# Graph network, first layer: one gather in 18 groups fetched row by row from ScalarE's queue

## The chip, the cores and the metric

One core of one Trainium2 chip runs the kernel. Times are device microseconds (us) of one execution; the time of a kernel is the median over its runs. The engines are PE (TensorE), DVE (VectorE), ACT (ScalarE), POOL (GpSimd) and SP (SyncE). A DMA is issued by SP, ACT or POOL and carried out by 16 DMA engines that they share.

## The reference

A graph of 6250 nodes with 128 features and 200,000 edges, sorted by destination. The change is in the first layer:

```python
h = x @ W1 + b1
e = concatenate([h[dst], h[src] - h[dst]])        # per edge, 256 wide
m = relu(e @ W2 + b2)
m = relu(m @ W3 + b3)
out = relu(segment_max(m, dst))
x = layernorm(x + out)
```

Two graph attention convolutions over the same edges follow (the "second layer" below, two passes), with softmax weights per destination, and another layernorm.

## The kernel before, in words

`e @ W2` splits into a part of the destination, P = h (W2a - W2b) + b2, and a part of the source, Q = h W2b. Both are made once per node; Q lies in HBM as `Q_table`, one row of 512 bytes a node. Then the edges are worked off in chunks of 128: 1563 chunks in 197 groups of 8 (the last three are smaller), and each group in two quads of 4 chunks, 391 quads in all (`groups`, `quads`). Three groups of six quads are a round; 64 rounds are full.

For each chunk the rows Q[src] must come into `q_ring`, which has three slots of a group each (group g uses slot g % 3).

- POOL (`gather_q`) gathers a chunk with one indirect DMA of 128 rows (line 485). Before group g it waits until PE has placed the last quad of group g-3 (`placed`).
- For the last chunk of every third group (`q_picks`, slot 2) there is no gather. PE picks its rows out of Q by products with one-hot matrices, from codes that ACT makes (`code_row`) and one-hots that DVE makes, in pieces spread over the round (`pick_piece`).
- SP (`load_windows`) loads for each chunk a window of 128 rows of P, 64 KB, into `w_ring`. It reads four window starts into registers (line 334) and issues four DMAs (line 338). Each adds 16 to `w_landed` of the slot.
- PE, in quad i: `place(i)` transposes the rows of Q into PSUM and adds the windows times a one-hot matrix; it waits for `q_landed` and `w_landed` of the whole group. Then `multiply(i-1)` by W3, then `turn_back(i-2)`, the transposes after the running maximum. In front of `multiply(i-1)` ACT must have made the ReLU of quad i-1.
- ACT, in quad i: `relu_quad(i)` (line 648), in the last quad of a round `code_row`, in every even quad the load of the ranks of a later group (line 663, 512 KB) and the store of a finished group (line 669, 512 KB), then `evacuate(i-2)` (line 655).
- DVE makes the one-hots and runs the maximum along the edges (`scan_quad`).

ACT's program is written out quad by quad. PE's runs rounds 2 to 62 in one hardware loop whose semaphore values are computed in registers.

The second layer already has row fetches of this kind, on SP: `fetch_rows` reads up to 12 row numbers into registers (line 377) and issues one DMA for each row into `one_rows` (line 381); when all 128 have landed, `move_rows` copies them into the ring with one DMA.

Of the kernel before, what the change touches and what calls it, by code (L numbers as in the profile page):

```python
# [7 lines left out]
I32 = mybir.dt.int32  # L8
# [4 lines left out]
P = 128  # L13
# [25 lines left out]
def totals(slots, amounts):  # L39

    so_far, out = {}, []
    for slot, amount in zip(slots, amounts):
        so_far[slot] = so_far.get(slot, 0) + amount
        out.append(so_far[slot])
    return out


def edge_network(nc, t, out):
    N, F = t["x"].shape
    L = t["src"].shape[1]  # L50
    NB = -(-N // P)
    NP = NB * P
    FULL, REST = N // P, N % P

    G, RING, RINGB, RINGO, AHEAD = 8, 3, 4, 3, 2
    G1, RING1, PIECE = 8, 3, 7
    PIECES = -(-NB // PIECE)
    W = F + 2
# [3 lines left out]
    groups, groups1 = cut(L, G, 4), cut(L, G1, 5)  # L62
# [15 lines left out]
    with ExitStack() as ctx:  # L78
        def sb(name, shape, dt=F32):
            return ctx.enter_context(nc.sbuf_tensor(name, shape, dt))  # L80

        def sem(name):
            return ctx.enter_context(nc.semaphore(name))
# [12 lines left out]
        src_row = sb("src_row", [P, 3, P], I32)  # L96

        one_src, one_rows = sb("one_src", [1, P], I32), sb("one_rows", [P, W])
        x_sb = sb("x_sb", [P, NB, F])

        work = sb("work", [P, NP + 7 * 512])
# [95 lines left out]

        q_picks = {RING * r + RING - 1: r - 2 for r in range(2, ROUNDS)}
        NQPICK = len(q_picks)
        pieces_after = {1: (0, 1), 2: (2,), 3: (3, 4), 4: (5,), 5: (6,)}  # L200
        by_product = [g for g, (j0, j1) in enumerate(groups1) if j1 - j0 == G1 and g >= 2]
        picks = {g: i for i, g in enumerate(by_product)}
# [5 lines left out]
        assert SHARE * (TURN - 1) >= P and all(g in picks for g in by_row) and TURN % RING1 == 0  # L208


        q_value = totals([g % RING for g in range(NG)], [16 * (j1 - j0 - (g in q_picks)) for g, (j0, j1) in enumerate(groups)])
        w_value = totals([g % RING for g in range(NG)], [16 * (j1 - j0) for j0, j1 in groups])
        b_value = totals([g % RINGB for g in range(NG)], [16] * NG)
        o_value = totals([g % RINGO for g in range(NG)], [16] * NG)
        by_dma = [(j0, j1 - (g in picks) - (g in by_row)) for g, (j0, j1) in enumerate(groups1)]
# [28 lines left out]
        h_landed = [sem(f"h_slot{i}") for i in range(RING1)]  # L244
        row_landed = [sem(f"src_row{i}") for i in range(3)]
        one_ready, one_landed = sem("one_ready"), [sem(f"one_rows{i}") for i in range(2)]

        tabs_stored, compact_zeroed, p_scattered, ranks_stored = (
            sem(n) for n in ("tabs_stored", "compact_zeroed", "p_scattered", "ranks_stored"))
# [204 lines left out]
        def pool_program(pool):  # L454
# [25 lines left out]
            def gather_q(g):  # L480
                j0, j1 = groups[g]
                if g >= RING:
                    pool.wait_ge(placed, last_of[g - RING] + 1)
                for j in range(j0, j1 - (g in q_picks)):
                    pool.indirect_dma_start(  # L485
                        out=q_ring[:, g % RING, j - j0, :], out_offset=None, in_=Q_table,
                        in_offset=bass.IndirectOffsetOnAxis(ap=srcT_i[:, j:j + 1], axis=0)).then_inc(q_landed[g % RING], 16)
# [77 lines left out]
        def scalar_program(scalar):  # L565
# [60 lines left out]
            def load_q_row(at):  # L626

                if at >= 2:
                    scalar.wait_ge(coded, at - 1)
                j = (RING * (at + 3)) * G - 1  # L630
                scalar.dma_start(src_row[:, row_slot[at], :], flat_src[j:j + 1, :].to_broadcast([P, P])).then_inc(row_landed[row_slot[at]], 16)
# [18 lines left out]
            def evacuate(i):  # L650
                g, a, n = quads[i]
                if a == 0 and g >= RINGO:
                    scalar.wait_ge(o_stored[g % RINGO], o_value[g - RINGO])
                scalar.wait_ge(turned_back, i + 1)
                scalar.activation(o_ring[:, g % RINGO, a:a + n, :],  # L655
                                  ps[4 + i % 2][:, 0:n * P].rearrange("p (c f) -> p c f", f=F), ACT.Copy).then_inc(evacuated, 1)
# [9 lines left out]
            def store_max(g):  # L666
# [2 lines left out]
                scalar.dma_start(run_max.rearrange("(c p) f -> p c f", p=P)[:, j0:j1, :],  # L669
                                 o_ring[:, g % RINGO, 0:j1 - j0, :]).then_inc(o_stored[g % RINGO], 16)  # L670

            scalar.wait_ge(ranks_stored, 32)
            scalar.wait_ge(q_low, PIECES)
            for g in range(RINGB):
                load_ranks(g)
            load_q_row(0)
            load_q_row(1)
            scalar.wait_ge(p_scattered, 16 * NB)
            for i in range(NQ + 3):
                turn, step = divmod(i, ROUND)  # L680
                if i < NQ:
                    relu_quad(i)
                    if step == ROUND - 1 and turn < NQPICK:
                        code_row(turn)
                    if step == 0 and 1 <= turn < NQPICK - 1:
                        load_q_row(turn + 1)
                    if quads[i][1] == 0 and RINGB <= quads[i][0] + AHEAD < NG:
                        load_ranks(quads[i][0] + AHEAD)
                if i >= 3 and last_of[quads[i - 3][0]] == i - 3:
                    store_max(quads[i - 3][0])  # L690
                if 2 <= i < NQ + 2:
                    evacuate(i - 2)

            def root(at, n):

# [535 lines left out]
        def tensor_program(tensor):  # L1231
# [66 lines left out]
            def place(q, count, i, landed, loaded, added):  # L1298

                g, a, n = quads[q]  # L1300
                if q >= 2:
                    tensor.wait_ge(relued, count[i - 1])
                tensor.wait_ge(q_landed[g % RING], landed)
                tensor.wait_ge(w_landed[g % RING], loaded)
                tensor.wait_ge(onto_made, count[i + 1])
                if g in q_picks and a + n == G:
                    tensor.wait_ge(row_added, added)
                for c in range(n):
                    piece = ps[q % 2][:, c * P:(c + 1) * P]
                    tensor.matmul(piece, lhsT=q_ring[:, g % RING, a + c, :], rhs=ident[:, :], start=True, stop=False, is_transpose=True)  # L1310
                    m = tensor.matmul(piece, lhsT=w_ring[:, g % RING, a + c, :], rhs=onto[:, q % 3, c * P:(c + 1) * P],  # L1311
                                      start=False, stop=True)
                m.then_inc(placed, 1)
# [48 lines left out]
            for i in range(ROUND, 2 * ROUND):  # L1362
                step(i)
                for c in pieces_after.get(i - ROUND, ()):
                    pick_piece(c, c + 1, None)
            with tensor.Fori(2, ROUNDS - 1) as turn:
                loaded, fewer = tensor.snap(turn * (16 * G) + 16 * G), tensor.snap(turn * (16 * G - 16) + 16 * (G + 1))
                added, made = tensor.snap(turn - 1), tensor.snap(turn * PIECES - PIECES)
                at = tensor.snap(turn * ROUND)
                count = {c: tensor.snap(at + c) for c in range(-3, ROUND + 1)}  # L1370
                for p in range(ROUND):
                    q = 2 * ROUND + p
                    place(q, count, p, fewer if quads[q][0] in q_picks else loaded, loaded, added)
                    multiply(q - 1, count, p - 1)
                    turn_back(q - 2, count, p - 2)
                    for c in pieces_after.get(p, ()):
                        pick_piece(c, made + (c + 1), added)
            for i in range(ROUND * (ROUNDS - 1), NQ + 2):
                step(i)

# [105 lines left out]
```

## Time and profile before

| | |
|---|---|
| median of 3 runs | 5880.39 us (5874.37 to 5883.29) |
| the profiled execution | 5872.45 us, its span 5871.2 us |
| first layer's gathers (line 485) | 1501, the last one at 2037.34 us |
| granted TensorE clock, mean | 0.94 of full speed |
| busy | PE 84%, DVE 70%, POOL 75%, ACT 45% of the span |

The span is the time from the first instruction to the last; the execution's own time holds a little more. Durations come from this one execution. Busy shares don't count register, semaphore and DMA-issuing instructions; on the queues (ACTq, SPq) these are shown in rows of their own. "issue" is time in which an engine waited for nothing that the profile shows.

### The profile page before, as it was taken

Reading aid. Unit: us, or ns where it says so; the run is one execution under the profiler, and the core shown is the slowest. Engines: PE = TensorE matmul, PEld = TensorE weight load, DVE = VectorE, ACT = ScalarE, POOL = GpSimd, SP = SyncE. Lnnn points to the kernel's source line nnn. Section 1 sums busy time; section 2 is a strip of 40 time slices with the busy share of each in tenths; the row PEclk is TensorE's granted clock in tenths of the full one; section 3 lists DMA queues with packets and bytes.
Section 4 is the critical chain, followed back from the end, with each engine's and each line's share of the span. In section 5 each row is a group of like instructions: output and inputs, shape, how many; then the busy total and the mean of one; then the engine's idle time right before and its main releaser. Section 6 shows DMA issues by size and latency. Waiting matters only on the chain.

```text
span 5871.2 us, 119756 instructions
## 1 busy us (share of the span) xinstructions
PE 4931.6 (84%) x29429; PEld 3060.9 (52%) x29429; DVE 4098.0 (70%) x10676; ACT 2658.7 (45%) x8225; POOL 4399.4 (75%) x4585
## 2 busy tenths in 40 slices
PE   3688888888888729999999999943999999999991
PEld 2566666666666525555555555522555555555550
DVE  4344454444445448888888888864888888888886
ACT  2233333333333235555555555533555555555554
POOL 7777777777777677777777777767777777777775
PEclk6899999999999959999999999976999999999995
DMA  6677777777777724444444444432444444444442
GB/s 157 187 219 217 215 223 216 217 219 217 220 217 216 202 59 120 123 124 122 124 125 124 125 124 124 125 92 63 124 123 124 124 125 124 124 124 121 125 125 83
DMA packets 808269, 874.81 MB, mean 149 GB/s; under 512 B 133438, under 2 KB 635185, under 8 KB 807818
## 3 DMA queue, kind: packets, MB, share of 16 engines
q0 software_dynamic: 146016, 295.63, 19.7%
q1 hardware_dynamic: 390298, 361.70, 18.8%
q10 hardware_dynamic: 271504, 213.69, 13.9%
q14 instruction: 440, 3.60, 0.2%
q8 instruction: 11, 0.18, 0.0%
HBM read 536.74 MB, written 331.81 MB: 148 GB/s over the span
## 4 chain that ended last, share of the span: by engine, by line
POOL 51%; issue 21%; DVE 9%; PE 7%; DMA 6%; ACT 3%; DVEq 0%; POOLq 0%; SPq 0%; ACTq 0%
POOL ring_a L545 25%; POOL ring_a L485 22%; DMA ring_a<-H_table,src_i 6%; PE ps L1417 5%; DVE ring_b L1120 5%; ACT ring_a L746 2%; POOL ring_a L512 2%; POOL ad_edges L520 2%; POOL P_compact L498 1%; PE ps L1311 1%; DMA ring_a<-Q_table,src_i 1%; DVE ring_a L1074 1%; PE ps L1321 1%; DVE gz L1104 1%; DVE ring_b L1074 0%
## 5 line engine op out<-in xcount | busy, mean ns | idle before, releaser
L545 POOL DMA_INDIRECT ring_a<-H_table,src_i x2712 | 2588.2, 954 | 826.9 <-issue 755.9
L1417 PE MATMUL ps<-work,ring_a 128*128 128x390 bf16 x10752 | 1867.3, 330 | 238.5 <-DVE ring_a L1074 234.9
L485 POOL DMA_INDIRECT ring_a<-Q_table,src_i x1501 | 1432.8, 955 | 461.0 <-issue 453.0
L1417 PEld LDWEIGHTS ps<-work,ring_a 128*128 128x128 bf16 x10752 | 1015.8, 98 | 1065.2 <-DVE ring_a L1074 387.7
L1417 PE MATMUL ps<-work,ring_b 128*128 128x390 bf16 x8064 | 1407.7, 329 | 0.0
L638 ACT ACTIVATE code<-src_row,code_bias 128x128 int16<-128x128 int32 x2676 | 829.5, 389 | 1214.2 <-DVE ring_b L1074 1152.0
L1120 DVE SCALAR_TENSOR_TENSOR ring_b<-ring_b,gw,ring_a 128x129 f32<-128x129 f32 x3124 | 1092.0, 350 | 120.4 <-ACT ring_a L746 104.2
L948 DVE TENSOR_TENSOR_SCAN work<-ring_b,work,ps 128x512 f32<-128x512 bf16 x390 | 498.4, 1278 | 951.8 <-PE ps L1321 911.1
L1417 PEld LDWEIGHTS ps<-work,ring_b 128*128 128x128 bf16 x8064 | 787.0, 98 | 559.7
L746 ACT ACTIVATE ring_a<-ring_a,gw 128x129 f32<-128x129 f32 x3126 | 959.3, 390 | 0.0
L1074 DVE TENSOR_TENSOR ring_a<-code,ps 128x896 bf16<-128x896 int16 x1536 | 944.1, 615 | 1.2 <-issue 0.3
L648 ACT ACTIVATE work<-ps 128x512 f32<-128x512 f32 x391 | 233.4, 597 | 1091.1 <-PE ps L1311 1069.6
L1310 PE MATMUL ps<-ident,ring_a 128*128 128x128 f32 x1563 | 446.5, 286 | 321.1 <-issue 164.6
L1074 DVE TENSOR_TENSOR ring_b<-code,ps 128x896 bf16<-128x896 int16 x1152 | 706.8, 614 | 0.0
L1311 PE MATMUL ps<-work 128*128 128x128 f32 x3126 | 567.1, 284 | 0.0
L1311 PEld LDWEIGHTS ps<-work 128*128 128x128 f32 x3126 | 501.4, 202 | 3.6 <-issue 0.3
L1310 PEld LDWEIGHTS ps<-ident,ring_a 128*128 128x128 f32 x1563 | 228.8, 146 | 391.3 <-issue 342.0
L1321 PE MATMUL ps<-work,W 128*128 128x512 f32 (+1 forms) x782 | 423.3, 625 | 0.0
L655 ACT ACTIVATE tab_flat<-ps 128x512 f32<-128x512 f32 x391 | 232.1, 594 | 262.6 <-PE ps L1331 259.0
L1331 PEld LDWEIGHTS ps<-ident,work 128*128 128x128 f32 x1563 | 202.3, 145 | 222.3 <-issue 221.2
L1101 DVE TENSOR_TENSOR gz<-ring_a,ad_wide 128x8 f32<-128x8 f32 (+2 forms) x394 | 70.3, 178 | 301.0 <-DMA ring_a<-H_table,src_i 291.5
L740 ACT ACTIVATE gw<-gw 128x16 f32<-128x16 f32 (+2 forms) x394 | 85.0, 216 | 384.0 <-DVE gw L1114 384.0
(267 smaller groups left out, 3625.2 us busy)
## 6 DMA issues: line engine op xcount, KB each, us to landing
run_sum<-ring_b SPq DMA_DIRECT2D x388, 520.0 KB
work<-P_compact SPq DMA_DIRECT2D x1563, 64.0 KB
ring_b<-rank_rows ACTq DMA_DIRECT2D x194, 512.0 KB, 5.2
run_max<-tab_flat ACTq DMA_DIRECT2D x194, 512.0 KB
one_rows<-H_table SPq DMA_DIRECT2D x3840, 0.5 KB
ring_a<-H_table,src_i POOLq DMA_INDIRECT x2712
src_row<-in_srcL SPq DMA_DIRECT2D x384, 64.0 KB, 3.0
ring_a<-Q_table,src_i POOLq DMA_INDIRECT x1501
```

The costliest lines, as they stand in the source:

```text
L485: pool.indirect_dma_start(out=q_ring[:, g % RING, j - j0, :], out_offset=None, in_=Q_table, in_offset=bass.IndirectOffsetOnAxis(ap=srcT_i[ ...
L545: pool.indirect_dma_start(out=h_ring[:, g % RING1, j - j0, :], out_offset=None, in_=H_table, in_offset=bass.IndirectOffsetOnAxis(ap=src_i[ ...
L638: scalar.activation(code[:, c, :], src_row[:, row_slot[at], :], ACT.Identity, bias=code_bias[:, c:c + 1])
L648: scalar.activation(m1T[:, b, 0:n * P], ps[b][:, 0:n * P], ACT.Relu).then_inc(relued, 1)
L746: scalar.activation(h_ring[:, slot, i, 0:F + 1], h_ring[:, slot, i, 0:F + 1], ACT.Copy, scale=gw[:, par, 0, i:i + 1]).then_inc(scaled, 1)
L948: vector.tensor_tensor_scan(scanned[:, b, 0:n * P], b_ring[:, g % RINGB, 1, a * P:(a + n) * P], ps[2 + b][:, 0:n * P], initial, ALU.add, A ...
L1074: vector.tensor_tensor(hot_space[c // 4][:, c % 4, 0:k1 - k0, :], code[:, c:c + 1, :].to_broadcast([P, k1 - k0, P]), blocks_ps[:, 0:k1 - k ...
L1120: vector.scalar_tensor_tensor(out=r_ring[:, slot, i, 0:F + 1], in0=previous, scalar=gw[:, par, 1, i:i + 1], in1=h_ring[:, slot, i, 0:F + 1 ...
L1310: tensor.matmul(piece, lhsT=q_ring[:, g % RING, a + c, :], rhs=ident[:, :], start=True, stop=False, is_transpose=True)
L1311: m = tensor.matmul(piece, lhsT=w_ring[:, g % RING, a + c, :], rhs=onto[:, q % 3, c * P:(c + 1) * P], start=False, stop=True)
L1321: tensor.matmul(ps[2 + b][:, 0:n * P], lhsT=weights["W3"][:, :], rhs=m1T[:, b, 0:n * P], start=True, stop=True).then_inc(multiplied, 1)
L1417: m = tensor.matmul(ps[parity][:, 0:3 * W], lhsT=hot_space[c // 4][:, c % 4, k - k0, :], rhs=split[:, k, :, :].rearrange("p s f -> p (s f) ...
```

## The change

Nine groups, 18, 36, ..., 162 (`q_by_row`, all in slot 0), lose the gather of their last chunk. ACT fetches its 128 rows instead. `list_q_few` loads the chunk's 128 source numbers into one partition (`few_src`). Over the first 32 of the 36 quads of a turn of 18 groups, `fetch_q_few` reads four numbers into registers behind the quad's evacuation and issues four DMAs of one row each into `few_rows`. In quad 34 `move_q_few` waits for all 128 rows and copies them with one DMA of 64 KB into the slot of the ring, and the next turn's list is loaded. The copy counts on `w_landed`, so PE waits for it there. There is no tenth turn: from quad 324 on ACT does what it did.

Since the expected values of `q_landed` and `w_landed` of slot 0 now step once in six rounds, PE's loop of 61 rounds becomes three: rounds 2 to 5; 8 super turns of 6 rounds, nested; and rounds 54 to 62. The body (`round_of`) is the same, with two more values in registers.

```diff
+        few_src, few_rows = sb("few_src", [1, P], I32), sb("few_rows", [P, W])
...
+        QTURN, QROWS = 18, 4
+        QTURNS = RING * ROUNDS // QTURN
+        q_by_row = [QTURN * i for i in range(1, QTURNS)]
...
-        q_value = totals([g % RING for g in range(NG)], [16 * (j1 - j0 - (g in q_picks)) for g, (j0, j1) in enumerate(groups)])
-        w_value = totals([g % RING for g in range(NG)], [16 * (j1 - j0) for j0, j1 in groups])
+        q_value = totals([g % RING for g in range(NG)], [16 * (j1 - j0 - (g in q_picks) - (g in q_by_row)) for g, (j0, j1) in enumerate(groups)])
+        w_value = totals([g % RING for g in range(NG)], [16 * (j1 - j0 + (g in q_by_row)) for g, (j0, j1) in enumerate(groups)])
...
-                for j in range(j0, j1 - (g in q_picks)):
+                for j in range(j0, j1 - (g in q_picks) - (g in q_by_row)):
                     pool.indirect_dma_start(
...
+            def list_q_few(turn):
+
+                j = groups[q_by_row[turn]][1] - 1
+                scalar.dma_start(few_src[:, :], flat_src[j:j + 1, :]).then_inc(q_listed, 16)
+
+            def fetch_q_few(turn, e0):
+
+                g = q_by_row[turn]
+                if e0 == 0:
+                    scalar.wait_ge(q_listed, 16 * (turn + 1))
+                    if turn:
+                        scalar.wait_ge(w_landed[g % RING], w_value[g - QTURN])
+                _, row = nc.values_load_multi_w_load_instructions(
+                    few_src[0:1, e0:e0 + QROWS], engines=[scalar.engine], min_val=0, max_val=NP - 1,
+                    skip_runtime_bounds_check_because="sources are numbers of nodes")
+                for d in range(QROWS):
+                    scalar.dma_start(few_rows[e0 + d:e0 + d + 1, 0:F], Q_table[bass.ds(row[d], 1), :]).then_inc(q_few_landed, 16)
+
+            def move_q_few(turn):
+
+                g = q_by_row[turn]
+                scalar.wait_ge(q_few_landed, 16 * P * (turn + 1))
+                scalar.wait_ge(placed, last_of[g - RING] + 1)
+                scalar.dma_start(q_ring[:, g % RING, G - 1, :], few_rows[:, 0:F]).then_inc(w_landed[g % RING], 16)
...
+            list_q_few(0)
             scalar.wait_ge(p_scattered, 16 * NB)
...
                 if 2 <= i < NQ + 2:
                     evacuate(i - 2)
+                turn_q, p = divmod(i, 2 * QTURN)
+                if turn_q < QTURNS - 1 and p * QROWS < P:
+                    fetch_q_few(turn_q, p * QROWS)
+                if turn_q < QTURNS - 1 and p == 2 * QTURN - 2:
+                    move_q_few(turn_q)
+                    if turn_q + 1 < QTURNS - 1:
+                        list_q_few(turn_q + 1)
...
-            with tensor.Fori(2, ROUNDS - 1) as turn:
-                loaded, fewer = tensor.snap(turn * (16 * G) + 16 * G), tensor.snap(turn * (16 * G - 16) + 16 * (G + 1))
+
+            def round_of(turn, first, windows):
+
+                loaded = tensor.snap(turn * (16 * G) + 16 * G)
+                fewer = tensor.snap(turn * (16 * G - 16) + 16 * (G + 1))
...
-                    place(q, count, p, fewer if quads[q][0] in q_picks else loaded, loaded, added)
+                    g = quads[q][0]
+                    place(q, count, p, (first, loaded, fewer)[g % RING], loaded if g % RING else windows, added)
...
+            each = QTURN // RING
+            with tensor.Fori(2, each) as turn:
+                round_of(turn, tensor.snap(turn * (16 * G) + 16 * G), tensor.snap(turn * (16 * G) + 16 * G))
+            with tensor.Fori(1, QTURNS - 1) as super_turn:
+                with tensor.Fori(0, each) as i:
+                    within = tensor.snap(i * (16 * G) + 16 * G)
+                    round_of(tensor.snap(super_turn * each + i), tensor.snap(super_turn * (16 * G * each - 16) + within),
+                             tensor.snap(super_turn * (16 * G * each + 16) + within))
+            with tensor.Fori(each * (QTURNS - 1), ROUNDS - 1) as turn:
+                round_of(turn, tensor.snap(turn * (16 * G) + (16 * G - 16 * (QTURNS - 1))),
+                         tensor.snap(turn * (16 * G) + (16 * G + 16 * (QTURNS - 1))))
```

## Rows read from the trace of the kernel before

**Rows 1.** Page, 1: busy time of each engine, share of the span, instructions
```profile
PE 4931.6 (84%) x29429; PEld 3060.9 (52%) x29429; DVE 4098.0 (70%) x10676; ACT 2658.7 (45%) x8225; POOL 4399.4 (75%) x4585
```

**Rows 2.** Page, 4: the chain that ended last, by engine and by line
```profile
POOL 51%; issue 21%; DVE 9%; PE 7%; DMA 6%; ACT 3%; DVEq 0%; POOLq 0%; SPq 0%; ACTq 0%
POOL ring_a L545 25%; POOL ring_a L485 22%; DMA ring_a<-H_table,src_i 6%; PE ps L1417 5%; DVE ring_b L1120 5%; ACT ring_a L746 2%; POOL ring_a L512 2%; POOL ad_edges L520 2%; POOL P_compact L498 1%; PE ps L1311 1%; DMA ring_a<-Q_table,src_i 1%; DVE ring_a L1074 1%; PE ps L1321 1%; DVE gz L1104 1%; DVE ring_b L1074 0%
```

**Rows 3.** Groups of instructions on POOL, 400 to 1900 us
```profile
L485 POOL DMA_INDIRECT ring_a<-Q_table,src_i x1193 | 1137.2, 953 | 363.7 <-issue 360.9 <-PE ps L1311 2.7
```

**Rows 4.** Busy us of PE, PEld, DVE, ACT, POOL; clock, DMA share, GB/s
```profile
400.00:1900.00 1500.00, 1301.26 (x8149) 927.30 (x8148) 735.75 (x1039) 470.21 (x982) 1136.65 (x1193) 0.97 0.79 218
```

**Rows 5.** ACT, then POOL, in order of time, 503 to 511 us
```profile
504.26 0.60 ACT L648 ACTIVATE work<-ps 128x512 f32<-128x512 f32 x1 [2.13 <-PE ps L1311]
...
510.24 0.94 POOL L485 DMA_INDIRECT ring_a<-Q_table,src_i  x1 [0.30 <-issue]
```

**Rows 6.** POOL in order of time, where the first layer's gathers end
```profile
2037.34 0.94 POOL L485 DMA_INDIRECT ring_a<-Q_table,src_i  x1 [0.30 <-issue]
...
2051.42 0.95 POOL L512 DMA_INDIRECT ring_a<-run_max,end_i  x1 [11.90 <-DMA run_max<-tab_flat]
```

**Rows 7.** SP's register loads of line 334 (four values at a time)
```profile
L334 SPq TENSOR_LOAD <-pair x391: 294/300/1462, 168.7 to 2032.1; - x196
```

**Rows 8.** SP's register loads (twelve values) and row DMAs, lines 377 and 381
```profile
L377 SPq TENSOR_LOAD <-one_src x330: 991/1728/2073, 2224.6 to 5638.9; - x165
...
L381 SPq DMA_DIRECT2D one_rows<-H_table x3840: 224/228/302, 2226.6 to 5643.1; - x192
```

**Rows 9.** SP's queue in order of time, 2504 to 2510 us
```profile
2504.23 4.83 SPq L381 DMA_DIRECT2D one_rows<-H_table  x12
2509.37 0.36 SPq L368 DMA_DIRECT2D src_row<-in_srcL  x1
```

**Rows 10.** ACT's DMA issues of lines 663, 669 and 631, with time to landing
```profile
L663 ACTq DMA_DIRECT2D ring_b<-rank_rows x197: 366/367/1199, 109.9 to 2034.9; - x197
...
DMA to landing us min/median/max: 4.7/5.2/9.9
...
L669 ACTq DMA_DIRECT2D run_max<-tab_flat x197: 366/482/1541, 189.2 to 2048.2; - x197
...
L631 ACTq DMA_DIRECT2D src_row<-in_src x62: 352/352/1957, 112.6 to 1904.6; - x62
```

**Rows 11.** Groups on ACT, 400 to 1900 us
```profile
L648 ACT ACTIVATE work<-ps 128x512 f32<-128x512 f32 x312 | 186.3, 597 | 822.8 <-PE ps L1311 814.6 <-issue 8.1
L655 ACT ACTIVATE tab_flat<-ps 128x512 f32<-128x512 f32 x311 | 184.6, 594 | 208.7 <-PE ps L1331 206.6 <-issue 2.0
```

**Rows 12.** ACT in order of time (start, length; idle before it), 1027 to 1053 us
```profile
1027.96 0.60 ACT L648 ACTIVATE work<-ps 128x512 f32<-128x512 f32 x1 [3.07 <-PE ps L1311]
1028.04 0.37 ACTq L663 DMA_DIRECT2D ring_b<-rank_rows  x1
1028.45 0.48 ACTq L669 DMA_DIRECT2D run_max<-tab_flat  x1
1029.26 0.60 ACT L655 ACTIVATE tab_flat<-ps 128x512 f32<-128x512 f32 x1 [0.70 <-PE ps L1331]
1031.73 0.60 ACT L648 ACTIVATE work<-ps 128x512 f32<-128x512 f32 x1 [1.87 <-PE ps L1311]
...
1037.14 0.60 ACT L648 ACTIVATE work<-ps 128x512 f32<-128x512 f32 x1 [2.29 <-PE ps L1311]
...
1039.77 0.60 ACT L648 ACTIVATE work<-ps 128x512 f32<-128x512 f32 x1 [0.55 <-PE ps L1311]
...
1047.01 0.60 ACT L648 ACTIVATE work<-ps 128x512 f32<-128x512 f32 x1 [5.40 <-PE ps L1311]
...
1050.77 0.60 ACT L648 ACTIVATE work<-ps 128x512 f32<-128x512 f32 x1 [1.87 <-PE ps L1311]
```

**Rows 13.** PE in order of time, 1034 to 1036 us
```profile
1035.50 0.33 PE L1310 MATMUL ps<-ident,ring_a 128*128 128x128 f32 x1 [1.43 <-DMA ring_a<-Q_table,src_i]
```

More of the change, by code:

```diff
@@ L199, in edge_network @@
         NQPICK = len(q_picks)
+        QTURN, QROWS = 18, 4
+        QTURNS = RING * ROUNDS // QTURN
+        q_by_row = [QTURN * i for i in range(1, QTURNS)]
+        assert 2 * QROWS * (QTURN - 2) >= P and QTURN % RING == 0 and not any(g in q_picks for g in q_by_row)
         pieces_after = {1: (0, 1), 2: (2,), 3: (3, 4), 4: (5,), 5: (6,)}
@@ L246, in edge_network @@
         one_ready, one_landed = sem("one_ready"), [sem(f"one_rows{i}") for i in range(2)]
+        q_listed, q_few_landed = sem("q_listed"), sem("q_few_rows")
         tabs_stored, compact_zeroed, p_scattered, ranks_stored = (
```

## The prediction

> **What bounds the kernel now.** I read the page's busy times first, then the chain, then the stretch that the change touches. Over the whole span POOL is busy 75% and PE 84% [rows 1], which alone would point at PE. The chain says otherwise: 51% POOL and 21% "issue" against 7% PE, with the gathers of line 485, those that the change takes some away from, at 22% of the span [rows 2]. In the stretch from 400 to 1900 us POOL makes 1193 gathers, busy for 1137.2 us and idle before them for 363.7 us, of which 360.9 us are put down to "issue", the time in which it waited for nothing [rows 3]. So a gather costs (1137.2 + 363.7) / 1193 = 1.258 us, POOL is fully occupied, and it never waits for the release of a slot in the ring. PE is busy 1301 of these 1500 us (87%), DVE 49%, ACT 31%; the DMA engines 79% [rows 4]. The remaining 13% of PE is waiting for gathers to land.
>
> How far behind POOL can PE fall before POOL feels it? Group g+3 uses group g's slot, so its first gather wants the last placement of group g, which is told by the ReLU behind it. I laid the 391 ReLUs against the first gather of every group. The tightest place in the steady part is the one shown: the second ReLU of group 34 starts at 504.26 and group 37's first gather at 510.24 [rows 5]. That is 6.0 us of room; the median over the groups is 9.4 us. At the very end room falls to 2.6 us, but the change puts nothing there (its last row fetch is in quad 319 of 391).
>
> **What the change removes.** Nine indirect gathers on POOL, those of groups 18, 36, ..., 162: 9 x 1.258 = 11.3 us. Because POOL is without gaps, the time comes off the first layer's gather phase, provided ACT and PE keep within the ring's room. Behind the last gather (2037.34) POOL waits 11.90 us for the last store of run_max and starts the next gathers at 2051.42 [rows 6]; this tail and all that follows is unchanged and moves forward as a block.
>
> **What it adds on ACT.** In 32 of every 36 quads, for nine turns, ACT reads four row numbers into registers and issues four DMAs of 512 bytes. The trace of before has neither on ACT, so I price them by SP. A load of four values took 0.300 us in the median, 0.294 at least and 1.462 at most [rows 7]; twelve values took 1.73 us [rows 8]. A row DMA took 0.228 us, and twelve of them 4.83 us, so they are (4.83 - 0.23) / 11 = 0.418 us apart, register arithmetic included [rows 8, 9]. A fetch is then 0.05 + 0.30 + 4 x 0.418 = 2.0 us. Of the 391 loads behind [rows 7] 64 took over 0.6 us, and the mean of all is 0.43 us, which adds 0.13: I take 2.2 us. Low bound 2.0 us. High bound: every load at 1.46 us and a DMA at ACT's own 0.352 us of line 631 [rows 10] in place of 0.228 (so 0.54 apart): 1.5 + 2.2 = 3.7 us. I stay near the low end because the spreading of one row over 128 partitions costs as much to issue on ACT (0.352 us, [rows 10]) as on SP (0.36 us, [rows 9]), so the 0.228 us should carry over; only the load is without a row on ACT.
>
> **Is it hidden?** ACT's idle time in the stretch is 822.8 us before the ReLUs and 208.7 us before the evacuations, over 312 quads: 3.31 us a quad [rows 11]. DMA issues are not counted as busy and lie in it: 156 stores at 0.48, 156 rank loads at 0.37 and 52 row loads at 0.35 [rows 10] are 151 us, 0.48 us a quad. Left: 2.82 us a quad, or 101.6 us in a turn of 36; the turn also gets 1.26 us shorter, so 100.3 us. Needed: 32 x 2.2 = 70 us. The point at which ACT becomes the bound is 100.3 / 32 = 3.1 us a fetch.
>
> The order within a group matters too, as the fetch stands behind the evacuation and in front of the next ReLU. In one round the idle stretches ahead of the six ReLUs are 3.07, 1.87, 2.29, 0.55, 5.40 and 1.87 us [rows 12]. A fetch of 2.2 us fits into the long ones and overruns 0.55 by 1.6 us and 1.87 by 0.3. What is late then is that ReLU; `multiply` of its quad stands on PE behind the placement of the next quad, and for a group's second quad that is the next group's, which waits for its gathers. So the delay falls into PE's waiting (1.43 us before the first placement of a round, [rows 13]) and at worst into the ring's 6.0 us. I cost it at nothing; without that cover it would be 1.6 us in one quad of six.
>
> A rule speaks against the low price. The trace's load of four values took 0.300 us [rows 7]. The Trainium skill, "DMA: Bandwidth & Descriptors", section on latency and other measured facts, gives a floor of about 600 ns for a register load from a tensor. By the page the fetch would be 2.5 us and 32 of them 80 us of the 100, and the sum would still be -11.3 us; the trace is below that floor, and the row decides.
>
> **The other pieces.** Once a turn, in step 34, ACT issues a 64 KB move from few_rows to the ring and the next list: about 0.5 + 0.4 us, in a step without a fetch. The move is queued behind that step's rank load and store, 512 KB each. In the round shown they are issued at 1028.04 and 1028.45 and the move would follow the evacuation that ends at 1029.86, at about 1030.0 [rows 12]; the next group's first placement starts at 1035.50 [rows 13], or 1.3 us sooner with one gather fewer. The move thus has 4.2 us. Rank loads land in 4.7 to 9.9 us, median 5.2 [rows 10]; I expect it 1 to 2 us late, at worst 5.7, nine times in all, which still is under the ring's 6.0 us: nothing. The wait for the 128 rows stands in front of the move on ACT, with the next ReLU behind it; the last rows were asked for three quads (14 us) earlier, beyond any landing in [rows 10]. The list for the next turn has two quads to land. The 1152 row DMAs carry 0.6 MB in 1.5 ms; beside 218 GB/s [rows 4] that is nothing in bytes, and in the second layer POOL's gathers already run beside SP's row DMAs.
>
> PE's 61 looped rounds are now 4 + 8 x 6 + 9, with some five register operations more a round and eight more loop entries. No row prices an entry; PE's idle time is (1500 - 1301) / 52 = 3.8 us a round [rows 4], and the loop back now lies in front of a wait of 1.43 us [rows 13], which bounds it. Between nothing and 3.8 us it is free; I take nothing.
>
> **Sum.** 5871.2 (span) - 11.3 = 5859.9 us for a profiled execution; it took 5872.45 with what lies around the span. The median of the runs is 5880.39, 7.9 us above that, so I predict 5880.4 - 11.3 = 5869 us. What a measurement of this kernel can tell from no change is about 0.2%, 11.8 us: the gain is 0.19%, just at that bound.
>
> **Rivals.**
> - *Given back by lateness (no change).* If the moves land after the ring's room, or ACT's delays and the loop entries add up to more than 6 us of lag, POOL waits for a slot near each of the nine moves. For it: the move sits behind 1 MB. Against: even the worst landing above stays inside 6.0 us. Price: 1 us beyond the room at each of nine turns leaves -2 us, about 5878. The Trainium skill, same page, section on queues, rings and completion order, says descriptors of one queue are consumed in ring order on each engine, so the move does start behind them; no run here shows the order yet.
> - *ACT becomes the bound (slower).* Place: ACT between evacuation and ReLU, in the 54 rounds with fetches; it decides from 3.1 us a fetch on. At 3.4 us a turn needs 32 x 3.4 = 108.8 against 100.3 us, +8.5 - 1.3 = +7.2 a turn, nine times +65 us: 5945. At the high bound of 3.7 us, 18.1 - 1.3, nine times: +151 us. For it: loads of up to 1.46 us exist on SP, and none is seen on ACT. Against: 327 of the 391 loads on SP took about 0.3 us, and 2.2 us leaves 30 us a turn.
> - *The gather wasn't the bound (no change).* PE at 87% could take over. Against: POOL's only waits are "issue"; PE would need 3.8 us more a round.
>
> **How the numbers follow.** Full gain 0.73, given back or PE the bound 0.14, ACT the bound 0.13. In the full gain the expected 11.3 us lies so near to 11.8 that the measured gain falls on either side about evenly (0.39 beyond it, 0.34 within). Of the second case 0.13 is within, of the ACT case 0.12 slower. With small remainders: faster 0.40, same 0.46, slower 0.14. The range is 5861 (11.3 us and the 8 us by which the three runs lie apart) to 5888, which takes in the no-gain case and the start of ACT's.
>
> **What would show it.** L485 in the page: nine gathers fewer, still 1.258 us apart, and no wait of POOL on PE longer than 0.3 us between 250 and 1900 us. The first gather of the ends (2051.42 before) 11.3 us earlier, near 2040. ACT's loads near 0.3 us and a fetch near 2.2 us; ACT's idle time before the ReLUs down from 2.6 to about 0.9 us a quad. PE's waits naming the move some nine times. The prediction is wrong if the load on ACT takes over 1.2 us as a rule, if ACT's row DMAs are more than 0.7 us apart, or if POOL waits for PE around groups 21, 39, 57.

## The result, and the profile after

The changed kernel took 5866.7 us in the median (5862.9 to 5868.5, 20 runs), the kernel before 5876.67 us in the same measurement (5873.0 to 5883.3, 20 runs). The ratio is 0.9981, 95% interval 0.9975 to 0.9988: about 11 us faster by the ratio (7 to 15 us), 10.0 us by the two medians. The forecast was 11.3 us, and 5869 us from a median of before that three runs had put at 5880.4.

Lines of the page after, from its parts 1, 4 and 5 (busy time; the chain by engine; the gathers with their busy time, mean and the idle time before them), answering to [rows 1, 2]:

```profile
PE 4937.7 (84%) x29429; PEld 3065.0 (52%) x29429; DVE 4093.1 (70%) x10676; ACT 2651.2 (45%) x8225; POOL 4397.1 (75%) x4576
...
POOL 51%; issue 21%; DVE 9%; DMA 7%; PE 7%; ACT 3%; DVEq 0%; POOLq 0%; SPq 0%; ACTq 0%
...
L493 POOL DMA_INDIRECT ring_a<-Q_table,src_i x1492 | 1425.8, 956 | 457.8 <-issue 449.7
```

Nine gathers are gone, at an unchanged 956 ns; POOL and "issue" still make up 72% of the chain. POOL's group in the stretch from 400 to 1900 us, against [rows 3]:

```profile
L493 POOL DMA_INDIRECT ring_a<-Q_table,src_i x1193 | 1137.2, 953 | 363.8 <-issue 359.2 <-PE ps L1352 4.6
```

Busy times of PE, PEld, DVE, ACT, POOL in that stretch, clock, DMA share and GB/s, against [rows 4]:

```profile
400.00:1900.00 1500.00, 1312.94 (x8206) 937.74 (x8207) 740.77 (x1046) 469.10 (x993) 1136.54 (x1193) 0.97 0.81 219
```

POOL makes the same 1193 gathers in 1500 us and its idle time is, as before, the 0.30 us between two of them. PE does 11.7 us more work in the same time, since the same 1193 gathers now belong to some eight more chunks; the DMA engines go from 79 to 81%.

The two ends of the gather phase, from POOL's timeline (start, length, line; idle before it):

```profile
170.08 0.99 POOL L493 DMA_INDIRECT ring_a<-Q_table,src_i  x1 [0.30 <-issue]
```

```profile
2029.34 0.95 POOL L493 DMA_INDIRECT ring_a<-Q_table,src_i  x1 [0.30 <-issue]
2030.59 0.94 POOL L513 DMA_INDIRECT first_bounds<-bounds_table,dst_i  x1 [0.30 <-issue]
2044.46 0.94 POOL L520 DMA_INDIRECT ring_a<-run_max,end_i  x1 [12.92 <-DMA run_max<-tab_flat]
```

The span shrank from 5871.2 to 5867.0, by only 4.2 us, and the milestones say why. The phase (167.83 to 2038.59 before) now runs from 170.08 to 2030.59: 1870.8 against 1860.5 us, so 10.3 us shorter for 1476 instead of 1485 gathers, 1.2605 us each instead of 1.2598. The start of this execution was 2.3 us later, the tail to the next gathers (11.90 us of waiting before, [rows 6]) 1.0 us longer, and all that follows 2.7 us longer; none of these places was touched, and one profile of each kernel doesn't separate a few us. The 20 runs of each do. The phase starts at 170.08 and not at the first gather, since 16 gathers are made ahead of it, between 79 and 105 us, in both kernels.

What the trace of before could not show, the register load and the row DMA on ACT (duration in ns, min/median/max):

```profile
L692 ACTq TENSOR_LOAD <-few_src x288: 477/486/1597, 180.7 to 1699.8; - x144
...
L696 ACTq DMA_DIRECT2D few_rows<-Q_table x1152: 234/235/877, 181.4 to 1702.1; - x192
```

### The profile page after: what moved, and what is told of

The parts are those of the page before. It is cut to its first block, busy times and chain, and to the rows that moved or that the text cites. A ratio compares the mean times of both kernels' runs of the same rounds, so it can differ in the third digit from the quotient of the medians.

```text
span 5867.0 us, 123619 instructions
## 1 busy us (share of the span) xinstructions
PE 4937.7 (84%) x29429; PEld 3065.0 (52%) x29429; DVE 4093.1 (70%) x10676; ACT 2651.2 (45%) x8225; POOL 4397.1 (75%) x4576
## 4 chain that ended last, share of the span: by engine, by line
POOL 51%; issue 21%; DVE 9%; DMA 7%; PE 7%; ACT 3%; DVEq 0%; POOLq 0%; SPq 0%; ACTq 0%
POOL ring_a L553 26%; POOL ring_a L493 21%; DMA ring_a<-H_table,src_i 5%; DVE ring_b L1161 5%; PE ps L1475 4%; ACT ring_a L787 2%; POOL ring_a L520 2%; POOL ad_edges L528 2%; DMA ring_a<-Q_table,src_i 1%; POOL P_compact L506 1%; PE ps L1352 1%; PE ps L1381 1%; PE ps L1362 1%; DVE gz L1145 0%; DVE ring_a L1115 0%
```

## Experiments

Everything but the named edit is as in the changed kernel, if not said otherwise. Eight of the twelve runs fell on chips on which the kernel before itself took 7775 to 7879 us; they are told last, since there POOL doesn't bound the kernel.

**The removal alone.** ACT's block and the first list are taken out, and the windows' values go back to those of before; the nine chunks are computed from what lay in the slot.

```diff
-                turn_q, p = divmod(i, 2 * QTURN)
-                if turn_q < QTURNS - 1 and p * QROWS < P:
-                    fetch_q_few(turn_q, p * QROWS)
...
```

> The removal alone (nine gathers left out, the nine chunks computed from what another chunk left in the slot; nothing added on ACT; PE's three loops stay), for a chip on which the kernel before takes its usual time. Theory A (ACT's part is hidden): 9 x 1.258 = 11.3 us faster than before, like the changed kernel (10.0 us) within 3 us. Rival B (ACT's part gives some of it back): 14 us or more faster than before.

Measured: 5876.5 against 5887.9 us of before on that chip, ratio 0.9981 (0.9972 to 0.9990), 11 us. POOL's group, 400 to 1900 us:

```profile
L493 POOL DMA_INDIRECT ring_a<-Q_table,src_i x1191 | 1137.0, 955 | 363.2 <-issue 360.4 <-PE ps L1344 2.7
```

The removal alone gives what the whole change gives; the two intervals together leave 6 to 7 us open, and up to 16 us for the gain here, so the times by themselves don't shut out rival B's 14 us. POOL's group does: what it waited for PE is 2.7 us here and 4.6 us in the changed kernel, and a gather costs the same. So ACT's fetches, the moves and PE's waits for them take nothing visible back. PE's three loops are in this kernel too; the interval leaves them some 5 us at most.

**ACT's part alone.** This is the kernel before with ACT's part put in: all gathers and PE's one loop stay, and the moves go to a tile that nobody reads. Against the changed kernel the move reads:

```diff
-                scalar.dma_start(q_ring[:, g % RING, G - 1, :], few_rows[:, 0:F]).then_inc(w_landed[g % RING], 16)
+                scalar.dma_start(few_aside[:, :], few_rows[:, 0:F]).then_inc(q_moved, 16)
```

> ACT's part alone (all gathers stay, PE's one loop stays; list, 1152 row DMAs and nine moves to a tile that nobody reads), for a chip on which the kernel before takes its usual time. Theory A: no difference from before within 3 us. Rival B: 3 us slower or more.

Measured: 5886.8 against 5887.9 us, ratio 0.9997 (0.9988 to 1.0006, so 7 us faster to 4 us slower). POOL's group:

```profile
L494 POOL DMA_INDIRECT ring_a<-Q_table,src_i x1190 | 1137.3, 956 | 363.1 <-issue 360.7 <-PE ps L1353 2.4
```

No wait of POOL on PE beyond the usual gap: 1170 DMAs and 288 register loads on ACT are free here. Theory A holds in both halves, by the times together with POOL's waits. The gather phases of the three profiles on this chip are 1862.2 us for 1476 gathers (removal alone), 1874.1 for 1485 (fetch alone) and 1860.5 for 1474 (the next run): 1.2617, 1.2620 and 1.2622 us a gather. The cadence is one number whatever ACT does, until its room is used up.

**Further, to the edge: turns of 15 groups, five rows a fetch.** The last fetch of a turn takes what is left of the 128 rows, here three.

```diff
-        QTURN, QROWS = 18, 4
+        QTURN, QROWS = 15, 5
```

> The change taken a smaller step further: turns of 15 groups, fetches of 5 rows, so 11 gathers leave POOL in place of nine. Where POOL bounds, 11 x 1.258 = 13.8 us below before, 3.8 us below the changed kernel. A fetch of five rows about 0.75 + 0.2 + 0.64 + 4 x 0.42 = 3.2 us, 26 of 30 quads. By the room of 2.82 us a quad (84.6 - 1.3 = 83.3 us a turn, 83 needed) it stands just at the edge. The run with 12 groups and seven rows lost 352 us, far more than 15 turns x 13 us = 190 us, which asks whether a step of a long fetch is late by itself (theory C: a fetch longer than the idle stretch before the next ReLU delays PE, whatever the mean room). By A1: -13.8 us. By C: slower than the changed kernel, by 10 us or more, with POOL waiting for PE.

Measured: 5874.65 against 5887.9 us, ratio 0.9976 (0.9967 to 0.9985): 13 to 14 us, where 11 x 1.258 = 13.8 were forecast. The load of five numbers, and who waited for whom (total us, times, longest):

```profile
L692 ACTq TENSOR_LOAD <-few_src x286: 731/1316/3469, 178.6 to 1732.7; - x143
```

```profile
POOL ring_a L493 <- issue: 361.2, 1184, 0.3
...
PE ps L1362 <- ACT work L656: 63.0, 63, 2.6
...
PE ps L1351 <- DMA ring_a<-few_rows: 21.0, 10, 3.0
...
POOL ring_a L493 <- PE ps L1352: 2.1, 7, 0.3
```

The load is not 0.75 us, as I had assumed, but 1.3 in the median and 1.72 in the mean of the 286, which makes a fetch 3.95 us. Still POOL waits for PE no more than its ordinary gap. But `multiply` on PE (line 1362) now waits 63 times for the ReLU, which it did not do in the changed kernel, and the room between a group's last ReLU and the first gather that wants its slot is down to 4.6 us in the median and, in the steady part, 1.4 us at the tightest (9.4 and 6.0 in the kernel before). This is close to the edge.

Theory A1, whose room was 83 us a turn, fails here: 26 fetches of 3.95 us are 103 us, so by A1 this kernel would have lost some 200 us. Theory C holds by half: a long fetch does make PE wait, up to 2.6 us at a time, but the ring takes it up and nothing is lost.

The version is the best of those run, but its interval overlaps that of the changed kernel, so that the further 2.5 us are the arithmetic's and not shown by the times alone.

**Over the edge: turns of 12 groups, seven rows a fetch.**

```diff
-        QTURN, QROWS = 18, 4
+        QTURN, QROWS = 12, 7
```

> The change taken further: turns of 12 groups in place of 18 and fetches of 7 rows in place of 4, so 15 gathers leave POOL in place of nine. Where POOL bounds, 15 x 1.258 = 18.9 us below before, 7.5 us below the changed kernel. ACT's need in a turn of 24 quads: in the changed kernel a fetch of four rows took 2.6 us, of which the load of the numbers 0.67, the first DMA 0.64 and each further one 0.42; with seven rows about 1.0 + 0.2 + 0.64 + 6 x 0.42 = 4.3 us, and 128 / 7 = 18.3 of them 79 us. Theory A1 (room 2.82 us a quad, idle time less other issues): 24 x 2.82 - 1.3 = 66 us, so 13 us too much a turn, and 15 turns are about 190 us slower than the changed kernel. Theory A2 (the queue also issues while an activation runs, so the evacuation's 0.6 us and the codes are room): about 86 us, nothing lost, and the 18.9 us come out in full.

Measured: 6228.6 against 5876.2 us, ratio 1.0599 (1.0582 to 1.0617): 352 us slower. ACT's load, a piece of ACT's timeline (ACTq rows are its DMAs), and the waits:

```profile
L692 ACTq TENSOR_LOAD <-few_src x285: 1081/1762/4083, 178.5 to 2241.3; - x143
```

```profile
1021.00 0.60 ACT L663 ACTIVATE tab_flat<-ps 128x512 f32<-128x512 f32 x1 [0.53 <-issue]
1025.00 2.87 ACTq L696 DMA_DIRECT2D few_rows<-Q_table  x7
1027.97 0.60 ACT L656 ACTIVATE work<-ps 128x512 f32<-128x512 f32 x1 [6.38 <-issue]
1028.47 0.59 ACT L663 ACTIVATE tab_flat<-ps 128x512 f32<-128x512 f32 x1
1029.92 2.81 ACTq L696 DMA_DIRECT2D few_rows<-Q_table  x7
1032.84 0.60 ACT L656 ACTIVATE work<-ps 128x512 f32<-128x512 f32 x1 [3.78 <-issue]
```

```profile
PE ps L1362 <- ACT work L656: 313.2, 162, 4.4
POOL ring_a L493 <- PE ps L1352: 291.4, 95, 6.3
POOL ring_a L493 <- issue: 278.9, 883, 5.8
```

A load of seven numbers took 1.76 us in the median and 2.40 in the mean of the 285, not 1.0, and a fetch 5.35 us. Between 1021.60, where an evacuation ends, and 1032.84 ACT's engine works 1.1 us, on one ReLU and one evacuation; the rest is two fetches, and "issue" is what its ReLUs now wait for. PE's `multiply` waits for the ReLU 313 us in 162 quads, and POOL waits 291 us in 95 places for PE's release. ACT has become the bound.

The size gives an estimate of the room. Over quads 60 to 300, two ReLUs are 6.23 us apart in this kernel where a fetch stands between them and 4.26 where none does. With a fetch of 5.35 us, 0.88 us of ACT's other work lies outside the fetch. POOL's pace is about 4.8 us a quad, so a fetch has 4.8 - 0.9 = 3.9 us. That the sum closes (19 fetch quads x (6.23 - 4.83) less 5 others x (4.83 - 4.26) is 24 us a turn, measured (352 + 18.9) / 15 = 24.7) shows that ACT's quads carry the whole loss, but it is the same run. Another kernel's check is the turns of 15 groups: 3.95 + 0.88 = 4.83 us, where the ReLUs are 4.82 us apart: just POOL's pace. So A2's mechanism stands and A1's room (3.1 us a fetch, that of the prediction) does not. In size A2's forecast failed for this run too, and for two reasons. The load was priced too low: 19 fetches of 5.35 us are 102 us a turn, which against A2's room of 86 us would have been some 215 us slower than before. And the room was smaller than that: 102 - 24.7 = 77 us a turn, about 4 us for each of the 19 fetches, since two ReLUs without a fetch between them are still 4.26 us apart and lend little.

**Chips on which the kernel before takes 7775 us or more.** There were three, A, B and C (7775, 7879 and 7778 us). The loops alone are the three `Fori` of PE with the values of before; eight and six rows are the changed kernel with more DMAs in a fetch:

```diff
                     scalar.dma_start(few_rows[e0 + d:e0 + d + 1, 0:F], Q_table[bass.ds(row[d], 1), :]).then_inc(q_few_landed, 16)
+                for d in range(4):
+                    scalar.dma_start(few_more[e0 + d:e0 + d + 1, :], Q_table[bass.ds(row[d], 1), :]).then_inc(q_more, 16)
```

> The removal alone: the nine gathers are left out and nothing takes their place (the nine chunks are computed from rows that another chunk left in the slot); no list, row DMA or move on ACT; PE's three loops stay. Theory A (ACT's fetches and the moves are fully hidden, POOL's 1.258 us a gather is all that counts): 9 x 1.258 = 11.3 us faster than before, and the same as the changed kernel within 0.05%. Rival B (the fetches and late moves gave part of the gain back): faster than the changed kernel by more than 3 us, so 14 us or more below before.

> ACT's part alone: all gathers stay on POOL and PE keeps its one loop; ACT reads the lists, issues the 1152 row DMAs and the nine moves, but the moves go to a tile that nobody reads. Theory A: no difference from before, within 0.05% (3 us). Rival B: slower than before by what the fetches cost, 1 us a turn or more, 10 us and up. POOL's waits for PE would show it.

> PE's three loops alone, with the semaphore values of before: all gathers stay, ACT does nothing more. Theory A: no difference from before, within 0.05%, since PE waits 13% of the stretch for gathers. Rival (each of the some ten more loop entries stops PE for several us, beyond the ring's room): 5 us slower or more, with idle time of PE in front of line 1351 grown by it.

> The changed kernel with eight row DMAs in each fetch in place of four (the second four go to a tile that nobody reads). In the changed kernel a fetch took 2.6 us on ACT's queue, so 2.6 + 4 x 0.41 = 4.2 us here. Theory A1 (ACT's room is the idle time between its activations less its other issues, 3.1 us a fetch, as in the prediction): (4.2 - 3.1) x 32 x 9 = 317 us slower than the changed kernel, about 6180 us. Theory A2 (the queue issues while the activation ahead still runs, so the evacuation's 0.6 us and the 2.3 us of code activations a round are room too, 3.1 + 0.6 + 0.3 = 4.0 us a fetch): (4.2 - 4.0) x 288 = 58 us slower or less. In both ACT has hardly an idle stretch left before its ReLUs and POOL waits for PE.

> The kernel with eight row DMAs in each fetch again, for a chip on which the kernel before takes its usual time (5876 us; on the chip of the first four runs it took 7775 us). The numbers stand as they were: a fetch of 4.2 us; theory A1 (room 3.1 us a fetch) 317 us slower than the changed kernel, about 6180 us; theory A2 (room about 4.0 us a fetch, since the queue issues while the activation ahead still runs) at most 58 us slower, about 5925 us.

> PE's three loops alone, with the semaphore values of before (all gathers stay, nothing added on ACT), for a chip on which the kernel before takes its usual time. Theory A: no difference from before within 3 us. Rival: 5 us slower or more.

> Eight row DMAs in each fetch of the changed kernel, on a chip on which the kernel before takes its usual time. A fetch of 2.6 + 4 x 0.41 = 4.2 us, 32 of them 134 us a turn. The run with turns of 12 groups took 371 us more than its gathers ask, 24.7 us a turn, at 18.3 x 5.35 = 98 us of fetches; the room would so be 73 us in 24 quads, 3.05 us a quad, 110 us in 36. Theory A1 (room 2.82 us a quad, as in the prediction, 100 us): 34 x 9 = 309 us slower than the changed kernel. Theory A1' (3.05 us a quad): 24 x 9 = 220 us slower. Theory A2 (room about 4.0 us a fetch, 128 us): 58 us slower or less.

> Six row DMAs in each fetch of the changed kernel: 2.6 + 2 x 0.41 = 3.4 us, 32 of them 109 us a turn. Theory A1 (room 100 us a turn): 9 x 9 = 80 us slower than the changed kernel. Theory A1' (110 us): between nothing and 10 us slower, with POOL's waits for PE beginning. Theory A2: the changed kernel's time.

| kernel | chip | ratio to before on its chip | 95% interval |
|---|---|---|---|
| removal alone | A | 0.9974 | 0.9951 to 0.9997 |
| fetch alone | A | 1.0073 | 1.0044 to 1.0102 |
| loops alone, twice | A; C | 1.0014; 1.0009 | 0.9987 to 1.0042; 0.9987 to 1.0031 |
| six rows | C | 1.0098 | 1.0070 to 1.0126 |
| eight rows, three times | A; B; C | 1.0192; 1.0247; 1.0134 | 1.0163 to 1.0221; 1.0142 to 1.0352; 1.0107 to 1.0162 |

None of the forecasts in us can be held against these, as they suppose POOL as the bound. Here it isn't. SP's queue instructions at one line, and POOL's group from 400 to 1900 us, of the kernel with the loops alone:

```profile
L346 SPq FUSED_REGOPS  x1563: 2/37/1382, 193.1 to 2398.2; - x196
...
L346 SPq DMA_DIRECT2D work<-P_compact x1563: 2/333/1385, 193.3 to 2398.5; - x196
```

```profile
L493 POOL DMA_INDIRECT ring_a<-Q_table,src_i x1011 | 967.9, 957 | 533.8 <-issue 268.0 <-remote 244.7 <-PE ps L1344 21.1
```

Medians are as usual (0.037 and 0.333 us), but register arithmetic of 0.037 us takes over 0.5 us in 78 of the 1563 and up to 1.4; in the kernel before on the usual chip its longest took 0.051 us. The granted TensorE clock is lower too, 0.86 in the mean against 0.94. POOL makes 1011 gathers in the stretch in place of 1193 and waits for others half of its idle time ("remote" is an update that the trace can't assign). What slows these chips I can't say; no run was made on it. What these runs do show is the change's other side. The fetch alone, free on a usual chip, costs 0.7% here, about 57 us:

```profile
L494 POOL DMA_INDIRECT ring_a<-Q_table,src_i x987 | 954.4, 967 | 547.3 <-issue 261.8 <-PE ps L1353 195.7 <-remote 89.8
```

PE's wait for the ReLU in front of `multiply`, loops alone and then fetch alone:

```profile
PE ps L1354 <- ACT work L656: 112.1, 57, 4.4
```

```profile
PE ps L1363 <- ACT work L657: 178.7, 120, 4.5
```

With the fetches on ACT it is 179 us in 120 quads against 112 in 57. That this wait carries the 57 us is likely but not shown, as PE's other waits differ between the two as well. The cost grows with the number of DMAs: on chip A, where the fetch of four rows costs 0.7%, eight rows cost 1.0192 - 0.9974 = 2.2% over the removal alone; on chip C the intervals of six rows (1.0098) and eight (1.0134) overlap. The loops can't be told from nothing in either run. So the fetches are hidden by room, not free. On a usual chip the edge between 2.6 and 5.35 us is known from the turns of 15 and 12 groups alone; six and eight rows were not run on one.

## Why the prediction was right

**The bound and the removal.** Right. POOL's cadence times nine: 11.3 us forecast, 1 - 0.9981 = 0.19% or 11 us measured, and 11 us for the removal alone, which also answers the rival that the gather was not the bound. The chances for "faster" and "same" were about even since the forecast lay at 0.19% against a bound of 0.2% (the parts named for "same", 0.34 and 0.13, add up to 0.47 and not 0.46). The measured gain lies at that bound, with an interval of 0.12 to 0.25%, so that the side on which it falls is luck. Part of the agreement in us is luck as well: the base was 3.7 us too high, the difference of the medians 1.3 us smaller than forecast.

The sign "first gather of the ends 11.3 us earlier, near 2040" did not come out so: it starts at 2044.46, 7.0 us earlier, because that execution began the phase 2.3 us later and waited 1.0 us longer behind it.

One reading was stronger than its rows. The prediction says that PE's idle 13% is waiting for gathers to land. The waits of PE in the stretch of the kernel before (total us, times, longest) name a gather for 76 of the 199 us:

```profile
PE ps L1310 <- issue: 121.9, 52, 3.6
PE ps L1310 <- DMA ring_a<-Q_table,src_i: 76.0, 61, 2.3
```

The other 121.9 us stand without a releaser, once a round, almost all at one place of the round. At that place the trace of the changed kernel names landings (172.9 us in 98 places in all), so the reading is likely right; the rows before alone don't show it.

**The price of a fetch.** Forecast 2.2 us, bounds 2.0 and 3.7; measured 2.58 in the mean of 288, from the load's start to the last DMA's end. Two terms were too low. The load of four numbers took 0.486 us in the median and 0.67 in the mean, against SP's 0.30 and 0.43: 85 of the 288 took over 0.8 us, around 1.05. They are not spread by chance: 80 of them are among the 90 loads in the third and fifth quad of a round, where ACT issues a rank load and a store ahead, while no load of the 144 in the even-numbered places (second, fourth, sixth) took more than 0.71 us. Why the first quad of a round, which has the same two issues, was slow in only 5 of 54, no run shows. And the first row DMA behind a load took 0.48 us instead of 0.23, the others about as on SP (0.235 against 0.228). The Trainium skill's floor of about 600 ns for such a load ("DMA: Bandwidth & Descriptors", latency and other measured facts) is above the median here too and below the mean; loads of five and seven numbers lie well over it.

**The room.** This step was wrong, harmlessly. The prediction put the break-even at 3.1 us a fetch, by idle time less issues. Fetches of 3.95 us in the mean cost nothing in the turns of 15 groups, and the estimate from the turns of 12 is 3.9 us; since a fetch took 2.58, both numbers give the same time. The prediction counted the queue and the engine one after the other. The timeline of ACT after shows them side by side:

```profile
1003.26 0.97 ACT L646 ACTIVATE code<-src_row,code_bias 128x128 int16<-128x128 int32 x3
1004.05 0.47 ACTq L696 DMA_DIRECT2D few_rows<-Q_table  x1
...
1004.68 0.23 ACTq L696 DMA_DIRECT2D few_rows<-Q_table  x1
...
1005.94 0.60 ACT L656 ACTIVATE work<-ps 128x512 f32<-128x512 f32 x1
...
1006.44 0.40 ACTq L671 DMA_DIRECT2D ring_b<-rank_rows  x1
1006.88 0.47 ACTq L677 DMA_DIRECT2D run_max<-tab_flat  x1
1007.45 0.60 ACT L663 ACTIVATE tab_flat<-ps 128x512 f32<-128x512 f32 x1 [0.91 <-PE ps L1372]
1008.12 1.95 ACTq L696 DMA_DIRECT2D few_rows<-Q_table  x4
1010.16 0.60 ACT L656 ACTIVATE work<-ps 128x512 f32<-128x512 f32 x1 [2.11 <-PE ps L1362]
1010.65 0.59 ACT L663 ACTIVATE tab_flat<-ps 128x512 f32<-128x512 f32 x1
1010.84 1.64 ACTq L696 DMA_DIRECT2D few_rows<-Q_table  x4
1016.93 0.60 ACT L656 ACTIVATE work<-ps 128x512 f32<-128x512 f32 x1 [5.68 <-PE ps L1352]
```

The evacuation starts at 1007.45 and runs 0.60 us; the load of the fetch behind it started at 1007.47, and the first DMA at 1008.12. At 1010.65 the next evacuation again runs over the load. In the first rows, DMAs of a fetch go out at 1004.05 and 1004.68 while `code_row` runs from 1003.26 on. Here the waits and the issues are the queue's, the activation is the engine's, and the queue does not wait for its end.

For the same reason a sign that I named was no sign: ACT's idle time before the ReLUs was to fall from 2.6 to 0.9 us a quad. In the stretch from 400 to 1900 us, against [rows 11]:

```profile
L656 ACT ACTIVATE work<-ps 128x512 f32<-128x512 f32 x314 | 187.5, 597 | 865.0 <-PE ps L1352 709.0 <-PE ps L1362 90.6 <-issue 65.1
L663 ACT ACTIVATE tab_flat<-ps 128x512 f32<-128x512 f32 x315 | 186.7, 593 | 165.8 <-PE ps L1372 157.9 <-issue 6.0
```

It is 865.0 / 314 = 2.75 us. The fetch lies in the idle time, and DMA issues don't count as busy, so that it hides there. What changed is what ended the idle time: "issue" from 8.1 to 65.1 us, and PE's line 1352, 814.6 before, to 709.0.

**Order within the group.** Right in kind. In the timeline above the fetch's last DMA ends at 1010.07 and the ReLU due after it starts at 1010.16, though its last release, an instruction of PE's line 1362, had ended at 1009.33: it was 0.8 us late, half of the 1.6 us forecast for this place. The next waited 5.68 us again for PE. No wait of PE for a ReLU appears among the waits of the stretch.

**The move.** Right in kind and size. ACT issued it at 1027.86, and PE stood until it had landed:

```profile
1027.78 0.60 ACT L663 ACTIVATE tab_flat<-ps 128x512 f32<-128x512 f32 x1 [0.70 <-PE ps L1372]
1027.86 0.49 ACTq L703 DMA_DIRECT2D ring_a<-few_rows  x1
```

```profile
1034.57 0.32 PE L1351 MATMUL ps<-ident,ring_a 128*128 128x128 f32 x1 [1.98 <-DMA ring_a<-few_rows]
```

The waits of the stretch (total us, times, longest):

```profile
PE ps L1351 <- DMA ring_a<-few_rows: 14.4, 8, 2.4
...
POOL ring_a L493 <- PE ps L1352: 4.6, 15, 0.3
```

Eight moves, 14.4 us, at most 2.4: 1.8 us late each, as forecast (1 to 2); the ninth lies before the stretch, at 344 us, and was waited for 1.6 us. This one landed 6.6 us after its issue, behind 1 MB of rank load and store on the same queue; how much of that is queueing no run separates. POOL felt nothing of it, its waits on PE being the ordinary gap. But the room shrank: the tightest place is group 90, the one with the move of 1027.86. Its second ReLU, and group 93's first gather:

```profile
1042.86 0.60 ACT L656 ACTIVATE work<-ps 128x512 f32<-128x512 f32 x1 [3.09 <-issue]
```

```profile
1045.32 0.94 POOL L493 DMA_INDIRECT ring_a<-Q_table,src_i  x1 [0.30 <-issue]
```

2.5 us, where the kernel before had 6.0 at its tightest, the removal alone 6.2 and ACT's part alone, for whose moves PE doesn't wait, 5.3. In group 90 two things meet: the 1.98 us for the move, and a fetch in front of this ReLU whose load took 1.36 us. The rival "given back by lateness" was 2.5 us away.

**The loops.** Nothing, as forecast, as far as a bound of 5 us tells (removal alone, whose loops are the changed ones).

**ACT as the bound.** The rival was real, only its threshold was about 0.8 us too low: with 5.35 us a fetch it cost 352 us.

## What to carry to other kernels

A saving on the engine whose idle time is all "issue" came out one to one here, so price the removed instructions by their cadence and look elsewhere only for what must stay hidden. For an engine that takes work over, the room is its pace less the work that its queue can't overlap: measure it as the distance of two of its instructions with a known load between, since idle time in the profile already holds the issues. And read the ring's slack at its tightest group, not in the mean: an addition that moves no time can still take most of it.

## What was not expected of the hardware

- A register load from SBUF on ACT took 0.486 us for four numbers, 1.316 for five and 1.762 for seven (medians; the slowest 1.60, 3.47 and 4.08). On SP, four took 0.300 and twelve 1.728 [rows 7, 8]. The count alone does not explain it. The loads of four always begin at a multiple of four in the list, those of five and seven mostly don't. A last load of a turn in the kernel with 15 groups, three numbers from place 125 on, took 0.882 us (all eleven of them 0.867 or more), longer than four numbers usually take, and a load of five from place 60 on took 0.731. Of the 198 loads of five that begin elsewhere than at a multiple of four none took less than 1.28 us. Where a load begins is thus a second candidate beside how much it reads, and no run separates the two. These two loads (duration in ns, start):

```profile
L692 ACTq TENSOR_LOAD <-few_src x1: 882/882/882, 1156.1 to 1156.1; - x1
```

```profile
L692 ACTq TENSOR_LOAD <-few_src x1: 731/731/731, 1382.4 to 1382.4; - x1
```

- The first row DMA behind such a load took 0.48 us on ACT, each further one 0.235.
- On some chips the kernel before took a third more time, with queue instructions of 0.037 us that at times took 1.4 us. The same added work that is free on a usual chip cost 0.7% there.
